# First graph layer: the messages' weights read from PSUM, and the score sum moved one step later

## What is computed

```python
h_all = einsum('nf,rof->rno', x, W)                      # 8 relations, 8 heads x 32
h_src, h_dst = h_all[edge_type, src], h_all[edge_type, dst]
scores = (h_src * attn_src).sum(-1) + (h_dst * attn_dst).sum(-1)
scores = where(scores > 0, scores, 0.2 * scores)
w = exp(scores - segment_max(scores, dst)[dst])          # softmax over the edges of a node
w = w / segment_sum(w, dst)[dst]
out = segment_sum(h_src * w[..., None], dst)             # 100000 edges, sorted by dst
```

## Time and profile before

| | us |
|---|---|
| median of 3 runs | 2919.15 |
| lowest and highest | 2917.01, 2926.32 |
| span of the profiled execution | 3121.8 |
| of it, the stage `attend0` | about 1368 (334 to 1702) |

### The profile page before, as it was taken

How to read it: one execution, slowest core, us unless ns; L and a number is a source line. 1 busy time by engine, 2 the same in 40 slices (tenths; PEclk the granted TensorE clock), 3 DMA queues, 4 the chain that set the end, 5 groups by cost and what they waited for, 6 DMA issues and landing times. The chain is left out here.

```text
span 3121.8 us, 48238 instructions
## 1 busy us (share of the span) xinstructions
PE 2116.7 (68%) x12946; PEld 1603.8 (51%) x12947; DVE 1814.9 (58%) x4412; ACT 1365.4 (44%) x3062; POOL 1640.8 (53%) x1492
## 2 busy tenths in 40 slices
PE   8999117576566666556655637954133599999998
PEld 5555105344444444444444626743132389999997
DVE  5422227666666666666667772355578686556565
ACT  4454125455455455455453214422133564444443
POOL 0066646777777777777771305544540155555554
PEclk9999557866777777777778557778555599999999
DMA  7677534444444444444442614565342063232332
GB/s 233 203 268 274 162 89 119 123 125 125 119 132 120 121 128 127 123 127 122 121 115 58 168 70 116 126 152 137 80 93 64 28 188 48 47 47 46 48 48 27
DMA packets 188418, 364.33 MB, mean 117 GB/s; under 512 B 44334, under 2 KB 120725, under 8 KB 181582
## 3 DMA queue, kind: packets, MB, share of 16 engines
q0 software_dynamic: 78160, 187.31, 25.9%
q1 hardware_dynamic: 106126, 171.10, 17.2%
q10 hardware_dynamic: 3968, 3.98, 0.5%
HBM read 247.26 MB, written 117.28 MB: 117 GB/s over the span
## 5 line engine op out<-in xcount | busy, mean ns | idle before, releaser
L833 POOL DMA_INDIRECT sum_ring<-h_tab,gnn_edge_row x880 | 913.2, 1038 | 396.8 <-issue 250.7
L1105 PE MATMUL sum_bank<-sum_ring,sum_one_hot 128*128 128x264 f32 x1760 | 647.1, 516 | 265.5 <-DVE nodes_acc L969 109.4
L1105 PEld LDWEIGHTS sum_bank<-sum_ring,sum_one_hot 128*128 128x128 f32 x1760 | 416.8, 253 | 416.6 <-issue 339.2
L877 ACT ACTIVATE sum_one_hot_T<-sum_distance,sum_pick_unit 128x1024 f16<-128x1024 bf16 x110 | 126.3, 1148 | 507.6 <-remote 503.1
L2202 POOL DMA_INDIRECT out_dram<-moe_y,slots_nodes x112 | 193.8, 1730 | 258.2 <-ACT moe_y L2224 241.2
L962 DVE TENSOR_TENSOR sum_ring<-sum_ring 128x1024 f32<-128x1024 f32 x220 | 267.6, 1217 | 66.7 <-ACT sum_ring L905 40.8
L884 ACT ACTIVATE sum_distance_by_lane<-all_iota,gnn_minus_local 128x128 bf16<-128x128 f32 x880 | 267.4, 386 | 0.1
L2376 PE MATMUL moe_bank<-moe_w_high,slots_early 128*128 x896 | 245.8, 274 | 6.1 <-DVE moe_w_low L1707 6.1
L2376 PE MATMUL moe_bank<-moe_w_low,slots_early 128*128 x896 | 245.7, 274 | 0.0
L2376 PE MATMUL moe_bank<-moe_w_high,moe_hidden_low 128*128 x896 | 245.6, 274 | 0.0
L969 DVE TENSOR_TENSOR nodes_acc<-sum_bank,nodes_acc 128x264 f32 x440 | 186.7, 424 | 98.0 <-remote 58.2
(11 more groups left out here) (444 smaller groups left out, 4562.6 us busy)
## 6 DMA issues: line engine op xcount, KB each, us to landing
h_tab<-rows_h_rows SPq DMA_DIRECT2D x49, 1056.0 KB
sum_local_rows<-local_tab SPq DMA_DIRECT2D x110, 256.0 KB
slots_stage<-in_L_ffn_W_dram SPq DMA_DIRECT2D x14, 1024.0 KB
sum_ring<-h_tab,gnn_edge_row POOLq DMA_INDIRECT x880
mask_tab<-rows_masks POOLq DMA_DIRECT2D x7, 1560.0 KB
sum_masks<-mask_tab SPq DMA_DIRECT2D x28, 390.0 KB
results<-moe_tiles SPq DMA_DIRECT2D x80, 128.0 KB
g_tab<-gnn_rows_out SPq DMA_DIRECT2D x49, 132.0 KB
```

What stands on the lines that cost most here:

```text
L833: nc.gpsimd.indirect_dma_start(ring[:, t % (RING * ST), :], None, k.h_tab, bass.IndirectOffsetOnAxis(k.edge_row[:, t:t + 1], 0)).then_inc( ...
L1105: last = nc.tensor.matmul(sum_b[j][:, 0:W0], hot[:, m % 3, t, :], ring[:, m % RING * ST + t, :], start=(u == 0), stop=(u == G - 1))
```

## The change

Three things change, all of them in `attend0`.

1. `messages` takes its weights from PSUM (`w_b`) instead of from the last columns of `ring`. ACT still copies them into `ring`, because the sums need them there, and the messages still wait for that copy. Since `w_b` is now read until the window's last message, `turn_weights` of the next window waits for those messages (`msg_ok`).
2. `rescale` no longer takes its factor from `w_b`. PE's `spread_fade` writes it to `side_b`, columns 258 to 265 (`GAIN`); it waits until the carry columns of `side_b` are read (`carry_c_ok`), and the next `turn_scores`, which writes `side_b`, waits until the factor is read (`gain_ok`). `turn_scores` therefore moves on PE from the start of its iteration to behind `pick(n + 1)`.
3. `add_src` moves on DVE from the end of iteration n to iteration n + 1, behind both messages and two of the adds.

```diff
+GAIN = GE + 2
...
-                by = ring[:, t0:t0 + ST // 2, D:W0].rearrange("p t (h o) -> p t h o", o=1).broadcast_to([P, ST // 2, H0, HD0])
+                c0 = (m % WS0 * ST + half * ST // 2) * H0
+                by = w_b[:, c0:c0 + ST // 2 * H0].rearrange("p (t h o) -> p t h o", h=H0, o=1).broadcast_to([P, ST // 2, H0, HD0])
                 nc.vector.tensor_tensor(to, to, by, ALU.mult).then_inc(msg_ok, 1)
...
-                nc.vector.tensor_scalar(gain[:, :], w_b[:, GE:GE + H0], 1.0, None, ALU.add).then_inc(gain_ok, 1)
+                nc.vector.tensor_scalar(gain[:, :], side_b[:, GAIN:GAIN + H0], 1.0, None, ALU.add).then_inc(gain_ok, 1)
...
                 if late:
                     add(m * SG - 3, old[1])
+                if 0 < n <= STEPS0:
+                    add_src(n - 1)
                 if scoring:
                     keep(n)
...
-                if scoring:
-                    add_src(n)
                 if n in turn_at:
...
                 pe.wait_ge(scored, min((w + 1) * WS0, STEPS0))
                 if w:
                     pe.wait_ge(carry_c_ok, w)
+                    pe.wait_ge(gain_ok, w)
...
                 pe.wait_ge(exp_ok, w + 1)
                 if w:
-                    pe.wait_ge(gain_ok, w)
+                    pe.wait_ge(msg_ok, w * WS0 * 2)
...
-                nc.tensor.matmul(w_b[:, GE:GE + H0], hot[0:1, m % 3, 0, :], fade[0:1, :], start=True, stop=True).then_inc(gain_ps, 1)
+                pe.wait_ge(carry_c_ok, w + 1)
+                nc.tensor.matmul(side_b[:, GAIN:GAIN + H0], hot[0:1, m % 3, 0, :], fade[0:1, :], start=True, stop=True).then_inc(gain_ps, 1)
...
-                if n in turn_at:
-                    turn_scores(turn_at[n])
...
                 if n + 1 < STEPS0:
                     pick(n + 1)
+                if n in turn_at:
+                    turn_scores(turn_at[n])
                 if n in weigh_at:
                     turn_weights(weigh_at[n])
```

## The result

| | before | changed |
|---|---|---|
| median of 4 runs, us | 2922.74 | 2842.74 |
| lowest and highest | 2917.01, 2926.48 | 2833.33, 2845.29 |
| span of the profiled execution | 3121.8 | 2840.1 |

The ratio is 0.9734, with a 95% interval from 0.9713 to 0.9755: 80 us less. The forecast was 2840.6. So the forecast of the time held and that of the span did not; the step behind the miss is named under "step by step".

What follows compares the result with a forecast made beforehand. POOL's gathers were taken to bound the stage at 10.81 us a step. Timed: 2919.15 - 74 (part 1) - 0 (part 2) - 5.5 (drain) + 1 (start) = 2840.6 us, own range 2825 to 2862; span 2973.

Steps and rivals of the forecast that it cites:

- POOL sets the pace: Steady stretch: POOL's 8 gathers with their pauses need 10.81 us a step, 1081 us for the 100 steps.
- Part 1, -74 us: Messages with one source in PSUM no longer lengthen POOL's gathers: -74 us of a 78.0 us excess, bounds 0 and 78.
- Rival (c): Messages hold gathers by their length, not their second source, so part 1 gives nothing: 2914.6 us; chance 0.06.
- No change on DVE: Messages reading PSUM last as long as from SBUF: 1215 ns carried on from adds and `keep`, against 1217.
- Part 2, 0 in the timed run: Late `add_src` saves 70 us of POOL's 87 us waits when profiled, 0 timed, taking PE's late signals as the recording's.
- rival (a): PE's late signals exist without a profile too, so part 2 counts as well: 2771 us; chance 0.14.
- DVE's and PE's own pace, 10.2 us: Step without gathers: DVE busy 7.44 us plus 2.44 of waits not for gathers, with small ones some 10.2 us.
- rival (b): POOL's pause or gather is cheaper unrecorded, so only about half of part 1 counts: 2880 us; chance 0.09.
- Drain, -5.5 us: After the last landing, DVE waits for it in iteration 110 after its second add instead of in iteration 109: -5.5 us.
- Start, +1 us: First window's `turn_scores` stands behind `pick(5)`, sixteen products and their one-hot matrix: +1 us allowed.
- Part 3, 0: Factor in `side_b`: `turn_scores` may wait 1 to 3 us once in 4 steps, under a 10 us cover; priced at nothing.
- Rival (d): New place of `turn_scores` holds totals and DVE's `leaky` up to 5.65 us a window: slower, 2954 us; chance 0.05.

Runs made afterwards that it cites:

- the third run of before: The kernel before, unchanged, profiled once more on a third chip beside the changed kernel: 2926.76 us, 2916.33 in the seven runs beside it.
- six gathers: Changed kernel fetching six of a step's eight tiles from the ring's second round on: 2601.3 us; the same with `add_src` in its old place: 2606.86.
- the pair 2859.06 and 2876.77: Changed kernel plus two unused 512-element DVE products per summing step, second source in PSUM: 2859.06 us; the same with it in SBUF: 2876.77 us.
- the kernel with late signals: The kernel before, unchanged, run on another chip, where POOL waits for sums: 3117.40 us in 8 runs.
- the chip of 3117 us: Chip where the kernel before, unchanged, took 3117.40 us in 8 runs and 3120.55 in the 9 beside them.

## The prediction against the runs, step by step

**POOL sets the pace: right.** The 10.81 us a step are what the third run of before has (10.80), and with six gathers the step follows it down.

**Part 1, -74 us: right in size and in reason.** The excess fell from 79.0 to 9.1, by 69.9 us, and the time from the first gather to the last by 69.8. The mean gather is 741.07 / 775 = 0.956 us, inside the 950 to 960 ns that were said. The twentieth that I left for short instructions with two SBUF sources was a little small: 9 us stay, not 4. The Trainium skill (SBUF — State Buffer, "Who interferes with whom") gave both rules. The lock taken by an instruction with two SBUF inputs is what the pair 2859.06 and 2876.77 shows. Its remark that `tensor_tensor` was not seen to stall DMAs doesn't hold for the issue of these gathers, which one message holds for up to 1985 - 947 ns. Rival (c) falls.

**No change on DVE: right.** A message takes 1208 ns from PSUM and 1215 from SBUF.

**Part 2, 0 in the timed run: the number is right by luck.** The step that failed is the sentence "they are the recording's". Recording adds nothing that shows here: the profiled execution of the changed kernel took 2841.92 us, its others 2833 to 2845, and the kernel with late signals takes its 3117 us without a profile too. The rows of the profiled execution are like those of the chip of 3117 us, and its three timed runs are like those of the other chips. So the 202.6 us lie between two conditions; on which chip the first profile was taken is not known. The 87 us of POOL's waits were indeed not in the median, which is all that the sum used. From this follows the miss in the span, 2973 against 2840.1: of the 196.8 us between the two profiles of before, 128.4 are POOL's waits and 64.6 lie behind the stage. That last piece ends before 2377 us: what follows takes the same time in both within 1 us. My "it can't be the matrix-bound part" was right for the last 642 us, where I had looked, and I took it for everything behind the stage.

**The waits themselves: open.** On the chip of 3117 us the changed kernel didn't run. So rival (a), that there the late `add_src` takes them away as well, is neither shown nor refuted, and what makes PE's signals late there isn't known beyond PE's own pauses.

**DVE's and PE's own pace, 10.2 us: wrong.** The six gathers show 7.6 or less. I had added waits of 2.44 us a step to DVE's busy time as if they were its own; in the third run of before, without the late signals, they are gone. The cover for part 3 was thus thicker than priced, and rival (b) had no room: 10.10 us of POOL against 7.6.

**Drain, -5.5 us: right.** 50.3, 51.9 and 50.4 us in the changed kernel against 56.0 and, with `add_src` put back, 57.1 and 57.3, so 4 to 7.

**Start, +1 us: not seen.** The step from ring filling to the steady stretch has no pause in either kernel; the 4.8 us in the table are before the first gather, where nothing was changed.

**Part 3, 0: right, with its wait undersized.** PE's waits at `turn_scores` in the changed kernel:

```profile
its engine sat idle before it (us, times) until:
  issue: 108.0, 27
  DVE sum_gain L1036: 105.1, 27
  DVE sum_score L954: 14.8, 2
```

105.1 / 27 = 3.9 us a window for the factor, where I had 1 to 3 (the 108.0 are the weight loads' share of the same waits). It ends no wait of POOL. It is in part an old wait in a new place: in the third run of before PE stood 61.0 us at `turn_scores` for the scores and 133.3 us behind it, at L1118, for the scans; at that second place it stands 6.1 us now. What it would cost without the cover is not shown, 105 us at most. Rival (d) needed a pace of DVE and PE above 9.4 us, and it is 7.6 or less.

**The sum: right, and closer than it deserved.** It says 78.5 us less. Measured were 80.0, 71.7 and 68.9 in three comparisons, and the traces explain 74. That the forecast lies 2 us from the first median is in part luck: part 1 gave 4 us less than said, and about 6 of the first 80 are not the change's by the traces.

## What to carry over

Where GpSimd's gathers set the pace, look at their longest ones and at what VectorE ran beside them: a VectorE instruction with both sources in SBUF holds a gather that starts within it until it is done, and moving one small source to PSUM gave back nearly all of it here. Before a wait in a profile is priced, compare the span with the timed runs; if they differ by 200 us, profile the kernel a second time before explaining the difference. Work added to an engine that is covered in the steady stretch still costs its full length in the drain.

## What the runs showed of the hardware

- An indirect gather of 128 rows takes 0.947 us and 0.305 us of pause at the median, beside all that PE and ACT do and beside most of DVE's work. One that starts within a `tensor_tensor` with two SBUF sources ends 0.82 us behind that instruction's end, 1985 ns at most in the third run of before; two such instructions in a row held one for 3089 ns. In all this was 79 of 2925 us.
- With one source in PSUM, `tensor_tensor` is not slower: 1208 against 1215 ns for 1024 elements, 677 against 681 ns for 512.
- The same kernel has medians of 3117 and 3121 us on one chip and of 2916 to 2923 on the others. On the chip of 3117 us 849 us of waits end by signals whose sender the profile doesn't show, PE also stands between its products for no wait shown, and the granted clock over the span is 0.778 against 0.811.
